# Measuring, rooting and first applying the next stage's layer norms inside each attention of the second layer

## The chip, the cores and the metric

The kernel runs on one core of one Trainium2 chip. The metric is the device time of one execution in microseconds (us). TensorE (PE) multiplies, VectorE (DVE), ScalarE (ACT) and GpSimd (POOL) do the rest, and SyncE (SP) issues transfers. Each engine works its own queue in order and meets the others at semaphores.

## The reference

Two pre-norm layers on x of 2 sequences x 2048 tokens x 256 features, float32. The first layer (16-head causal attention, then a mixture of 8 experts with two chosen) is not touched by the change. The second layer is

```python
x = x + _L1_attn_ref(_layernorm(x), L1_attn_W)      # returns n + softmax(causal(n K^T)) V, with K, V = n @ W.T and n the normed x
x = x + _L1_ffn_ref(_layernorm(x), W1, b1, W2, b2)  # relu(n @ Wq1.T + b1) @ Wq2.T + b2, the weights quantized to -1, 0, 1
```

with `_layernorm(x) = (x - mean) / sqrt(var + 1e-5)` over the 256 features of a token.

## The kernel before

x stays in SBUF as `X`, 32 rows of tiles: tile t holds 128 tokens, 16 tiles per sequence, in 4 blocks of 4 tiles (512 tokens). The second layer runs as five stages, each a block of the program behind a barrier of all engines:

1. keys of sequence 0 (`phase_keys(k, 0)`), 2. its attention (`phase_attend(k, 0)`), 3. keys of sequence 1, 4. its attention, 5. the MLP over the 8 blocks of both sequences (`phase_mlp`).

**A layer norm of a block** is made in three steps by three helpers. `norm_measure` (L224, L227): four BN_STATS and four BN_AGGR on DVE, which give mean and variance of the four tiles. `norm_root` (L233): one Sqrt on ACT. `norm_apply` (L239, L242): a reciprocal and four TENSOR_SCALARs on DVE, which write the normed tiles `xn`. Then PE turns them (8 transposes, L158, `turn`), ACT copies the result's high part out of PSUM (L165, `high_parts`) and DVE subtracts it for the low part (L171, `low_parts`); the matmuls take high and low parts.

**Keys of sequence 1.** For each block i PE multiplies the keys (12 matmuls into `ps_k`), turns block i+1, and multiplies the values (24 matmuls into `ps_v`). DVE's order is: norm 0, low parts 0, norm 1, and then for each i: low parts of the keys (L1872), low parts of the turned block i+1, the whole norm of block i+2. PE's turn of block i+2 waits for that norm. POOL adds the normed block into `X` (`residual`, L1791) and makes the low parts of the values (L1761). SP loads the key and value weights (`kv_hi`, `kv_lo`; PE waits for both before the first key matmul) and after them the MLP's raw weights. In sequence 0 ACT applies all blocks but the first; that stage is left as it is.

**Attention.** For each query tile q the scores are cut in parts of up to 4 key tiles. PE turns the first two parts of q's probabilities, multiplies the scores of q+1, and then weighs the values with q's parts. ACT makes the exponentials (L2060) and the high parts of the turned probabilities (L2069). DVE makes their low parts (`lows`, L2027), then the maxima of tile q+1's scores (`soften`, L2015 to L2022), in sequence 1 one step of the MLP's weight quantization (`ternary`), the row sum and its reciprocal, and at last adds the attended tile into `X` (L2049). In sequence 0's attention POOL adds the expert results into `X` for the 16 tiles of sequence 1.

**MLP.** It begins with the norm of block 0. In block i, ACT first takes the root of block i+1's norm, which waits for DVE's measurement, and then makes 8 high parts of the hidden layer (L2193) after a wait for the biases' load; DVE makes the full hidden values (L2222), POOL the low parts (L2176).

ACT holds the functions of one table set at a time; a load of another set is an instruction of its own (ACT_TABLE_LOAD). Exp and Sqrt lie in different sets here.

Of the kernel before, what the change touches and what calls it, by code (L numbers as in the profile page):

```python
# [15 lines left out]
P = 128  # L16
# [191 lines left out]

def layer_norm(k, mem, stem):


    nc = k["nc"]
    norm = {"X": k["X"], "eps": k["eps"], "k": k}
    for name, shape in (("stats", [P, 2, TB, 6]), ("moments", [P, 2, TB, 2]), ("std", [P, 2, TB]), ("rstd", [P, 2, TB])):
        norm[name] = mem.enter_context(nc.sbuf_tensor(f"{stem}_{name}", shape, F32))
    for name in ("stats_ok", "moments_ok", "std_ok", "rstd_ok", "xn_ok"):
        norm[name] = sem(k, f"{stem}_{name}")
    return norm


# [15 lines left out]
def norm_apply(dve, w, b, j, out, first=0):  # L236

    dve.wait_ge(w["std_ok"], b + 1)
    dve.reciprocal(w["rstd"][:, j], w["std"][:, j]).then_inc(w["rstd_ok"], 1)  # L239
    dve.wait_ge(w["rstd_ok"], b + 1)  # L240
    for t in range(TB):
# [29 lines left out]
def phase_qkv(k):  # L271
# [3 lines left out]
    with ExitStack() as mem:  # L275
# [24 lines left out]
        ps_n = ps("ps_n", [P, BT])  # L300
        norm = layer_norm(k, mem, "ln1")

# [673 lines left out]
def phase_tokens(k):  # L976
# [10 lines left out]
    with ExitStack() as mem:  # L987
# [79 lines left out]

        norm = layer_norm(k, mem, "ln2")
        x_turn = turner(k, "x2_turn", ps_t)
# [645 lines left out]
def phase_keys(k, b):  # L1715
# [3 lines left out]
    with ExitStack() as mem:  # L1719
# [10 lines left out]
        if b:  # L1730
# [32 lines left out]
        with nc.Block() as block:  # L1763
# [23 lines left out]
            def _(pool):  # L1787
                def residual(i):
                    x = k["X"][:, T0 + TB * i:T0 + TB * i + TB, :]
                    pool.wait_ge(norm["xn_ok"], i + 1)  # L1790
                    pool.tensor_tensor(x, x, xn[:, i], ALU.add).then_inc(k["residual_ok"], 1)  # L1791

# [12 lines left out]
            def _(act):  # L1805
# [3 lines left out]
                def root(i):  # L1809

                    norm_root(act, norm, i, i % 2)
                    if i and not b:
                        norm_apply_act(act, norm, i, i % 2, lambda t: xn[:, i, t:t + 1, :], T0, i)
# [34 lines left out]
            def _(dve):  # L1848
                def normed(i):
                    j = i % 2  # L1850
                    if not b:
                        if i == 0:
                            add_routed(dve, 0)
                        dve.wait_ge(sum_ok, 2 * i + 2)
                    norm_measure(dve, norm, i, j, T0)
                    if i and not b:
# [33 lines left out]
            def _(pe):  # L1890
                def turn(i):
                    pe.wait_ge(norm["xn_ok"], i + 1)
                    turn_block(pe, x_turn, i, lambda t, c: xn[:, i, t, c * P:(c + 1) * P])

# [25 lines left out]


CUTS = SEQ_TILES // 4
CUT = D * D_FF // P // CUTS


def phase_attend(k, b):

    nc, io = k["nc"], k["io"]
    with ExitStack() as mem:
# [3 lines left out]
        def ps(name, shape, dt=F32):  # L1933
# [26 lines left out]
        with nc.Block() as block:  # L1960
# [31 lines left out]
            def _(dve):  # L1992
# [31 lines left out]
                def lows(n):  # L2024
# [28 lines left out]
            def _(act):  # L2053
# [18 lines left out]
                for q in range(SEQ_TILES):  # L2072
# [56 lines left out]
def phase_mlp(k):  # L2129
# [3 lines left out]
    with ExitStack() as mem:  # L2133
# [14 lines left out]
        ps_t, ps_h, ps_y = ps("ps_x4", [P, DC, BT]), ps("ps_h4", [P, 3, BT]), ps("ps_y4", [P, TB, D])  # L2148
        norm = layer_norm(k, mem, "ln4")
        x_turn = turner(k, "x4_turn", ps_t)  # L2150
# [4 lines left out]
        with nc.Block() as block:  # L2155
# [128 lines left out]
def program(nc, io):  # L2284
# [12 lines left out]
    with ExitStack() as ctx:  # L2297
# [41 lines left out]
        first_ctx.close()  # L2339
        third_ctx, third_sems = semaphores(k)  # L2340
        half = 0
        for b in range(BATCH):
# [15 lines left out]
        mlp = len(third_sems)  # L2358
        k["stale"] = third_sems[half:] + [k["first_in"]]
        phase_mlp(k)  # L2360
        with nc.Block() as block:

            @block.gpsimd
            def _(pool):
                clear(pool, third_sems[mlp:])

# [32 lines left out]
```

## Time and profile before

| | us |
|---|---|
| median of 3 runs | 1761.5 |
| lowest and highest run | 1756.29 and 1763.25 |
| the profiled execution | 1764.49 |
| its span, first to last instruction | 1762.6 |

| engine | busy us | share of the span |
|---|---|---|
| PE | 1613.9 | 92% |
| DVE | 953.4 | 54% |
| ACT | 946.1 | 54% |
| POOL | 447.2 | 25% |

The profile's mean granted TensorE clock is 0.958 of full speed. A row of the time line gives start, duration, engine, line, operation and tiles, and in brackets the engine's idle time just before it and what ended it. A row of several instructions of one kind ends in their count.

### The profile page before, as it was taken

The page shows a single profiled execution, that of the slowest core. Times are in us where ns is not written, and L with a number is a line of the kernel's source. Part 1 is how long each engine was busy: PE and PEld are TensorE (multiplying, and loading weights), DVE is VectorE, ACT ScalarE, POOL GpSimd, SP SyncE. Part 2 cuts the span into 40 slices and gives each one's busy share as a digit, 9 for nine tenths or more (in the row PEclk, how much of TensorE's full clock was granted, in tenths as well). Part 3 has the DMA queues.
Part 4 walks back from the last instruction along what each step waited for, and adds up shares of the span by engine and source line. Part 5 has one row for each costly group of instructions (what it writes and reads, how often), then busy time and mean ns, then how long its engine had stood idle before and what let it go on. Part 6 is the DMA issues. An engine that isn't in the chain of part 4 may idle for free. (4 is left out here: it accounts for less than half of the span.)

```text
span 1762.6 us, 30806 instructions
## 1 busy us (share of the span) xinstructions
PE 1613.9 (92%) x10249; PEld 1111.8 (63%) x10250; DVE 953.4 (54%) x1846; ACT 946.1 (54%) x1521; POOL 447.2 (25%) x495
## 2 busy tenths in 40 slices
PE   6979999999999959998799999999579986997998
PEld 5833333333333337887678888888468976896887
DVE  6726566665554456777423333333356555655785
ACT  4779999999999933444222222222143434343432
POOL 0111121121111113555312222222343013001665
PEclk9989999999999978999899999999789988998999
DMA  7882855954732057213631111111312020000001
GB/s 230 232 219 87 216 141 128 235 128 126 154 64 41 19 167 288 93 63 136 204 107 48 54 48 54 48 51 51 130 36 73 1 72 1 1 1 4 25 24 48
DMA packets 88019, 169.40 MB, mean 96 GB/s; under 512 B 13504, under 2 KB 47808, under 8 KB 84768
## 3 DMA queue, kind: packets, MB, share of 16 engines
q1 hardware_dynamic: 80728, 146.90, 29.7%
q0 software_dynamic: 7056, 20.95, 3.6%
q8 instruction: 67, 1.10, 0.3%
q14 instruction: 40, 0.33, 0.1%
q10 hardware_dynamic: 128, 0.13, 0.0%
HBM read 96.67 MB, written 71.26 MB: 95 GB/s over the span
## 5 line engine op out<-in xcount | busy, mean ns | idle before, releaser
L836 ACT ACTIVATE probs<-ps_s 128x1024 f32<-128x1024 f32 (+3 forms) x640 | 511.7, 938 | 11.3 <-PE ps_s L902 8.3
L919 PE MATMUL ps_o<-probs,V 128*17 128x512 f32 (+3 forms) x2560 | 293.0, 536 | 1.6 <-POOL probs L824 1.2
L824 POOL TENSOR_SCALAR_AFFINE_SELECT probs<-probs 128x512 f32<-128x512 f32 x128 | 96.9, 763 | 427.5 <-ACT probs L836 426.4
L1638 DVE COPY slot_hT<-ps_hT 128x512 f32<-128x512 f32 x71 | 49.1, 692 | 196.7 <-PE ps_hT L1680 196.7
L902 PEld LDWEIGHTS ps_s<-Q_even,K_even 50*128 50x128 f32 x640 | 55.4, 186 | 133.4 <-ACT probs L836 119.9
L1688 PE MATMUL ps_slot_y<-we_out,slot_hT 128*128 x568 | 136.5, 384 | 2.2 <-issue 1.3
L2176 POOL TENSOR_TENSOR h_lo<-h,h_hi 128x512 fp32r<-128x512 f32 x64 | 89.4, 1414 | 178.9 <-DVE h L2222 178.9
L902 PEld LDWEIGHTS ps_s<-Q_odd,K_odd 50*128 50x128 f32 x640 | 54.9, 183 | 123.2 <-ACT probs L836 117.4
L902 PE MATMUL ps_s<-Q_even,K_even 50*128 50x512 f32 (+3 forms) x640 | 123.7, 444 | 8.9 <-DMA Q_even<-shift_parts 7.9
L902 PE MATMUL ps_s<-Q_odd,K_odd 50*128 50x512 f32 (+3 forms) x640 | 122.8, 439 | 0.3
L1599 POOL DMA_INDIRECT routed_rows<-slot_y,home_row x71 | 69.3, 977 | 176.4 <-ACT slot_y L1618 171.0
L2060 ACT ACTIVATE probs<-ps_s,neg_row_max 128x512 f32<-128x512 f32 (+2 forms) x80 | 49.4, 624 | 119.9 <-DVE neg_row_max L2022 119.9
L1688 PEld LDWEIGHTS ps_slot_y<-we_out,slot_hT 128*128 128x128 f32 x568 | 103.5, 192 | 14.7 <-issue 3.1
L874 DVE RECIPROCAL inv_denominator<-inv_denominator 128x512 f32<-128x512 f32 x32 | 107.3, 3353 | 1.1
L919 PEld LDWEIGHTS ps_o<-probs,V 128*17 128x17 f32 x2560 | 44.7, 95 | 85.6 <-issue 55.3
L1613 ACT ACTIVATE slot_xT_hi<-ps_xT 128x256 fp32r<-128x256 f32 x71 | 27.3, 384 | 123.0 <-PE ps_xT L1667 123.0
L1618 ACT ACTIVATE slot_y<-ps_slot_y 128x256 f32<-128x256 f32 x71 | 27.3, 384 | 108.0 <-PE ps_slot_y L1688 108.0
L141 PE MATMUL ps_o<-v_hi,pT_hi 128*128 128x256 f32 x272 | 80.8, 297 | 2.2 <-DVE pT_lo L2027 2.0
L1623 ACT ACTIVATE slot_silu<-ps_slot_mid 128x512 f32<-128x512 f32 x71 | 42.5, 598 | 71.0 <-PE ps_slot_mid L143 71.0
L1649 DVE TENSOR_TENSOR slot_h<-slot_silu,ps_slot_gated 128x512 f32<-128x512 f32 x71 | 48.8, 688 | 57.6 <-PE ps_slot_gated L143 57.6
L872 DVE COPY inv_denominator<-ps_o 128x512 f32<-128x512 f32 x32 | 22.1, 692 | 104.2 <-PE ps_o L933 104.2
L142 PE MATMUL ps_o<-v_lo,pT_hi 128*128 128x256 f32 x272 | 77.4, 284 | 0.0
(274 smaller groups left out, 3959.0 us busy)
## 6 DMA issues: line engine op xcount, KB each, us to landing
weight_parts<-weight_hi SPq DMA_DIRECT2D x20, 512.0 KB, 4.4
weight_parts<-weight_lo SPq DMA_DIRECT2D x20, 512.0 KB, 5.1
we_hi<-weight_parts SPq DMA_DIRECT2D x19, 512.0 KB, 5.9
we_lo<-weight_parts SPq DMA_DIRECT2D x19, 512.0 KB, 13.2
slot_rows<-slots_in SPq DMA_DIRECT2D x71, 128.5 KB, 2.1
qk_parts<-qk_hi SPq DMA_DIRECT2D x32, 256.0 KB, 4.6
qk_parts<-qk_lo SPq DMA_DIRECT2D x32, 256.0 KB, 5.3
we_hi<-attended_parts SPq DMA_DIRECT2D x16, 512.0 KB, 7.9
```

The source lines that it names most:

```text
L141: pe.matmul(out, lh, rh, start=start, stop=False)
L142: pe.matmul(out, lh, rl, start=False, stop=False)
L824: pool.affine_select(out=block_of, in_=block_of, compare_op=ALU.is_ge, fill=0.0, base=0, pattern=[[0, HG], [1, P]], channel_multiplier=-1) ...
L836: act.activation(probs[:, at % PROB_BUFS, 2 * p:2 * p + 2, off:BT], ps_s[:, s % SCORE_BUFS, :, off:BT], ACT.Exp).then_inc(exp_ok, 1)
L874: dve.reciprocal(inv[:, :], inv[:, :]).then_inc(norm_ok, 1)
L902: last = pe.matmul(ps_s[:, s % SCORE_BUFS, h, off:BT], K[j][HALF * h:HALF * h + USED_ROWS, p, t * P:(t + 1) * P], Q[j][HALF * h:HALF * h + ...
L919: last = pe.matmul(ps_o[32 * h:32 * h + DH + 1, s % 2, off:BT], k["V"][:, group, SEQ_TILES * b + t, h, :], probs[:, at % PROB_BUFS, h, off ...
L1599: pool.indirect_dma_start(out=io["routed"], out_offset=bass.IndirectOffsetOnAxis(ap=home[:, j], axis=0), in_=y[:, j, :], in_offset=None).t ...
L1638: dve.tensor_copy(hT[:, :, :], ps_h[:, :, :]).then_inc(hT_ok, 1)
L1688: last = pe.matmul(ps_y[:, :], hT[:, f], wo[:, bass.ds(e, 1), f, :], start=(f == 0), stop=(f == FC - 1))
L2060: act.activation(probs[:, q % 2, g * P:(g + m) * P], ps_s[:, g * P:(g + m) * P], ACT.Exp, bias=neg_top[:, q:q + 1], accum_out=chunk_total[ ...
L2176: pool.tensor_tensor(h_lo[:, j, f], h[:, f % 2], h_hi[:, j, f].bitcast(F32), ALU.subtract).then_inc(lo_ok, 1)
```

## The change

The variances of the next stage's blocks are measured inside the attention, where DVE has one measurement per query tile from q = 9 on: four in sequence 0's attention (for the four blocks of sequence 1), one in sequence 1's (for the MLP's block 0). ACT takes one root over all of them after its work of q = 13. DVE makes the reciprocals and applies the norm to the first block at q = 14, into a buffer `next_xn` that lives across stages. The keys stage of sequence 1 then has no measurement and no root, and DVE only applies blocks 1 to 3; the MLP begins with PE's turn of block 0. The sums that POOL makes on sequence 1's tiles are waited for before each measurement.

```diff
+def norm_scale(dve, w, j, out, row):
+
     for t in range(TB):
-        last = dve.tensor_scalar(out(t), w["X"][:, bass.ds(first + TB * b + t, 1), :], w["moments"][:, j, t, 0:1],
+        last = dve.tensor_scalar(out(t), w["X"][:, bass.ds(row + t, 1), :], w["moments"][:, j, t, 0:1],
                                  w["rstd"][:, j, t:t + 1], ALU.subtract, ALU.mult)
     last.then_inc(w["xn_ok"], 1)
...
-        norm = layer_norm(k, mem, f"ln3_{b}")
+        norm = k["next_norm"] if b else layer_norm(k, "ln3", norm_space(k, mem, "ln3", 2))
+
+        def xn_of(i):
+            return k["next_xn"][:, :, :] if b and i == 0 else xn[:, i]
...
                 def root(i):
 
+                    if b:
+                        return
                     norm_root(act, norm, i, i % 2)
...
                 def normed(i):
                     j = i % 2
-                    if not b:
-                        if i == 0:
-                            add_routed(dve, 0)
-                        dve.wait_ge(sum_ok, 2 * i + 2)
+                    if b:
+                        if i:
+                            dve.wait_ge(norm["rstd_ok"], 1)
+                            norm_scale(dve, norm, i, lambda t: xn[:, i, t:t + 1, :], T0 + TB * i)
+                        return
...
+MEASURE_AT, ROOT_AT, APPLY_AT = 9, SEQ_TILES - 3, SEQ_TILES - 2
...
+        following_norm = k["next_norm"] = layer_norm(k, "ln4" if b else "ln3_next", k["next_space"][b])
+        AHEAD, next_row = (1, 0) if b else (SEQ_BLOCKS, SEQ_TILES)
...
+                def next_applied():
+
+                    w = following_norm
+                    dve.wait_ge(w["std_ok"], 1)
+                    dve.reciprocal(w["rstd"][:, 0:AHEAD], w["std"][:, 0:AHEAD]).then_inc(w["rstd_ok"], 1)
+                    dve.wait_ge(w["rstd_ok"], 1)
+                    norm_scale(dve, w, 0, lambda t: k["next_xn"][:, t:t + 1, :], next_row)
...
                     for n in OF[q][2:]:
                         lows(n)
+                    if 0 <= q - MEASURE_AT < AHEAD:
+                        if not b:
+                            dve.wait_ge(summed, TOP_K * (q - MEASURE_AT + 1))
+                        norm_measure(dve, following_norm, q - MEASURE_AT, q - MEASURE_AT, next_row)
+                    if q == APPLY_AT:
+                        next_applied()
                     if b:
                         ternary(q)
...
+                    if q == ROOT_AT:
+                        w = following_norm
+                        act.wait_ge(w["moments_ok"], TB * AHEAD)
+                        act.activation(w["std"][:, 0:AHEAD], w["moments"][:, 0:AHEAD, :, 1], ACT.Sqrt, bias=k["eps"][:, 0:1]
+                                       ).then_inc(w["std_ok"], 1)
...
             @block.scalar
             def _(act):
-                norm_root(act, norm, 0, 0)
                 high_parts(act, x_turn, 0, lambda c: xT_hi[:, 0, c])
...
             @block.vector
             def _(dve):
-                norm_measure(dve, norm, 0, 0)
-                norm_apply(dve, norm, 0, 0, lambda t: xn[:, 0, t:t + 1, :])
-
...
-                    turn_block(pe, x_turn, i, lambda t, c: xn[:, j, t, c * P:(c + 1) * P])
+                    rows = k["next_xn"] if is_first(i) else xn[:, j]
+                    turn_block(pe, x_turn, i, lambda t, c: rows[:, t, c * P:(c + 1) * P])
```

The rest of the diff hands semaphores and buffers over between stages.

DVE's queue from the end of sequence 0's attention into the keys of sequence 1, before (the first row is the last addition into X of the attention):

```order
L2049 SCALAR_TENSOR_TENSOR X<-ps_o,inv_row_sum,X 128x256
L1960 UNCONDITIONAL_BRANCH
L1847 UNCONDITIONAL_BRANCH
L224 BN_STATS ln_1_stats<-X 128x6 x4
L227 BN_AGGR ln_1_moments<-ln_1_stats 128x2 x4
L239 RECIPROCAL ln_1_rstd<-ln_1_std 128x4
L242 TENSOR_SCALAR xn<-X,ln_1_moments,ln_1_rstd 128x256 x4
L171 TENSOR_TENSOR q3T_lo<-ps_x,q3T_hi 128x512 x2
L224 BN_STATS ln_1_stats<-X 128x6 x4
L227 BN_AGGR ln_1_moments<-ln_1_stats 128x2 x4
L239 RECIPROCAL ln_1_rstd<-ln_1_std 128x4
L242 TENSOR_SCALAR xn<-X,ln_1_moments,ln_1_rstd 128x256 x4
```

and in the change, from the same row:

```order
L2089 SCALAR_TENSOR_TENSOR X<-ps_o,inv_row_sum,X 128x256
L1986 UNCONDITIONAL_BRANCH
L1866 UNCONDITIONAL_BRANCH
L171 TENSOR_TENSOR q3T_lo<-ps_x,q3T_hi 128x512 x2
L255 TENSOR_SCALAR xn<-X,next_keys_moments,next_keys_rstd 128x256 x4
L1895 TENSOR_TENSOR k3T_lo<-ps_k,k3T_hi 128x512 x2
L171 TENSOR_TENSOR q3T_lo<-ps_x,q3T_hi 128x512 x2
L255 TENSOR_SCALAR xn<-X,next_keys_moments,next_keys_rstd 128x256 x4
```

The stage now begins with the low parts of block 0's turned tiles, and each later block has its four TENSOR_SCALARs alone.

ACT's queue in the change, around q = 13 and 14 of sequence 0's attention (probs is the exponential, pT_hi the high part of the turned probabilities):

```order
L2100 ACTIVATE probs,chunk_sum<-ps_s,neg_row_max 128x512
L2100 ACTIVATE probs,chunk_sum<-ps_s,neg_row_max 128x384
L2124 ACT_TABLE_LOAD
L2124 ACTIVATE next_keys_std<-next_keys_moments,eps 128x16
L2109 ACTIVATE pT_hi<-ps_p 128x512 x2
L2100 ACT_TABLE_LOAD
L2100 ACTIVATE probs,chunk_sum<-ps_s,neg_row_max 128x512
```

The two loads and the root stand where before the exponentials were followed by the two high parts at once. The same three rows are new in sequence 1's attention, while the load and root at the start of the keys stage and the load at the start of sequence 1's attention are gone.

DVE's queue in the change, at q = 14 of sequence 1's attention:

```order
L2053 TENSOR_TENSOR pT_lo<-ps_p,pT_hi 128x512
L2053 TENSOR_TENSOR pT_lo<-ps_p,pT_hi 128x384
L2060 RECIPROCAL next_mlp_rstd<-next_mlp_std 128x4
L255 TENSOR_SCALAR next_xn<-X,next_mlp_moments,next_mlp_rstd 128x256 x4
L2028 TENSOR_SCALAR below<-w_raw,half_gamma 128x512
L2082 TENSOR_REDUCE row_sum<-chunk_sum 128x1
L2085 RECIPROCAL inv_row_sum<-row_sum 128x1
L2089 SCALAR_TENSOR_TENSOR X<-ps_o,inv_row_sum,X 128x256
L2053 TENSOR_TENSOR pT_lo<-ps_p,pT_hi 128x512 x4
```

The reciprocal and the four TENSOR_SCALARs are new; they stand ahead of the quantization step, the row sum and the addition into X.

## Rows read from the trace of the kernel before

**Rows 1.** Stretches: length, PE, PEld, DVE, ACT, POOL busy, clock, DMA share, GB/s
```profile
1434.00:1482.80 48.80, 33.63 (x178) 29.60 (x179) 29.95 (x72) 23.42 (x42) 19.89 (x13) 0.82 0.18 65
1482.80:1608.50 125.70, 118.40 (x784) 107.91 (x784) 76.50 (x192) 46.76 (x121) 0.00 (x0) 0.96 0.00 1
1608.50:1632.50 24.00, 13.38 (x48) 10.21 (x48) 16.26 (x40) 9.22 (x15) 9.69 (x7) 0.79 0.03 6
```

**Rows 2.** Time line, start of the keys stage of sequence 1
```profile
1434.62 1.28 ACT L233 ACT_TABLE_LOAD   x1 [3.28 <-PEq L1960]
1434.66 1.41 DVE L224 BATCH_NORM_STATS2 ln_stats<-X 128x6 f32<-128x256 f32 x4 [0.32 <-PEq L1960]
1436.21 0.38 DVE L227 BATCH_NORM_AGGREGATE ln_moments<-ln_stats 128x2 f32<-128x6 f32 x4
...
1437.17 1.38 DVE L242 TENSOR_SCALAR xn<-X,ln_moments,ln_rstd 128x256 f32<-128x256 f32 x4
...
1438.61 1.97 PE L158 MATMUL ps_x<-ident,xn 128*128 128x128 f32 x8 [4.79 <-DVE xn L242]
...
1442.68 0.77 PE L141 MATMUL ps_k<-q3T_hi,kv_hi 128*128 128x512 f32 x1 [2.10 <-DVE q3T_lo L171]
```

**Rows 3.** DMA issues at 1435.00 and 1609.19: KB, us from issue to landing
```profile
kv_lo<-weight_parts SPq DMA_DIRECT2D x1, 512.0 KB, 4.5
```
```profile
b_rows<-b SPq DMA_DIRECT2D x1, 128.0 KB, 3.0
```

**Rows 4.** Time line, PE, DVE and POOL at the turns of blocks 2 and 3
```profile
1457.78 1.10 PE L158 MATMUL ps_x<-ident,xn 128*128 128x128 f32 x8 [2.89 <-DVE xn L242]
1468.92 1.96 PE L158 MATMUL ps_x<-ident,xn 128*128 128x128 f32 x8 [2.90 <-DVE xn L242]
```
```profile
1453.64 4.08 DVE L242 TENSOR_SCALAR xn<-X,ln_moments,ln_rstd 128x256 f32<-128x256 f32 x4
...
1464.77 4.09 DVE L242 TENSOR_SCALAR xn<-X,ln_moments,ln_rstd 128x256 f32<-128x256 f32 x4
```
```profile
1451.86 2.71 POOL L1761 TENSOR_TENSOR v_lo<-v_raw,v_hi 128x512 fp32r<-128x512 f32 x2 [10.88 <-ACT v_hi L1841]
1454.53 2.40 POOL L1791 TENSOR_TENSOR X<-X,xn 128x1024 f32<-128x1024 f32 x1
```

**Rows 5.** Stretches of 1 us, PE alone: length, busy, granted clock, DMA
```profile
1458.00:1459.00 1.00, 1.00 (x10) 0.86 0.00 0
...
1462.00:1463.00 1.00, 1.00 (x10) 0.93 0.00 0
...
1472.00:1473.00 1.00, 1.00 (x9) 0.81 0.00 0
```

**Rows 6.** Time line, start of the MLP
```profile
1608.86 1.40 DVE L224 BATCH_NORM_STATS2 ln_stats<-X 128x6 f32<-128x256 f32 x4 [0.32 <-PEq L1960]
...
1612.80 1.97 PE L158 MATMUL ps_x<-ident,xn 128*128 128x128 f32 x8 [4.79 <-DVE xn L242]
...
1618.90 0.30 ACT L233 ACTIVATE ln_std<-ln_moments,eps 128x4 f32<-128x4 f32 x1 [3.01 <-DVE ln_moments L227]
...
1619.11 0.67 ACT L2193 ACTIVATE h_hi<-ps_h,b_columns 128x512 fp32r<-128x512 f32 x1
```

**Rows 7.** Time line, sequence 1's attention: DVE at q = 9 and q = 14, ACT at q = 14
```profile
1543.42 0.48 DVE L2049 SCALAR_TENSOR_TENSOR X<-ps_o,inv_row_sum,X 128x256 f32<-128x256 f32 x1
1544.49 1.29 DVE L2027 TENSOR_TENSOR pT_lo<-ps_p,pT_hi 128x512 fp32r<-128x512 f32 x2 [0.58 <-ACT pT_hi L2069]
...
1547.05 0.69 DVE L2017 TENSOR_REDUCE chunk_max<-ps_s 128x1 f32<-128x512 f32 x1 [0.67 <-PE ps_s L143]
...
1599.14 0.48 DVE L2049 SCALAR_TENSOR_TENSOR X<-ps_o,inv_row_sum,X 128x256 f32<-128x256 f32 x1 [0.93 <-PE ps_o L143]
```
```profile
1586.96 1.09 ACT L2069 ACTIVATE pT_hi<-ps_p 128x512 fp32r<-128x512 f32 x2 [1.11 <-PE ps_p L2103]
1594.30 0.69 ACT L2060 ACTIVATE probs<-ps_s,neg_row_max 128x512 f32<-128x512 f32 x1 [6.25 <-DVE neg_row_max L2022]
```

More of the change, by code:

```diff
@@ L206, in _, with norm_space, layer_norm @@
             dve.tensor_copy(k["head_sel"][:, :], k["head_sum"][:, :]).then_inc(picked, 1)
[L209 to L215, printed above, removed]
+def norm_space(k, mem, stem, blocks):
+    return {name: mem.enter_context(k["nc"].sbuf_tensor(f"{stem}_{name}", [P, blocks, TB] + shape, F32))
+            for name, shape in (("stats", [6]), ("moments", [2]), ("std", []), ("rstd", []))}
+def layer_norm(k, stem, space):
+    norm = {"X": k["X"], "eps": k["eps"], "k": k, **space}
     for name in ("stats_ok", "moments_ok", "std_ok", "rstd_ok", "xn_ok"):
@@ L218, in layer_norm, with norm_parts @@
     return norm
+def norm_parts(norm):
+    return [norm[name] for name in ("stats_ok", "moments_ok", "std_ok", "rstd_ok", "xn_ok")]
 def norm_measure(dve, w, b, j, first=0):
@@ L240, in norm_apply @@
     dve.wait_ge(w["rstd_ok"], b + 1)
+    norm_scale(dve, w, j, out, first + TB * b)
+def norm_scale(dve, w, j, out, row):
     for t in range(TB):
-        last = dve.tensor_scalar(out(t), w["X"][:, bass.ds(first + TB * b + t, 1), :], w["moments"][:, j, t, 0:1],
+        last = dve.tensor_scalar(out(t), w["X"][:, bass.ds(row + t, 1), :], w["moments"][:, j, t, 0:1],
                                  w["rstd"][:, j, t:t + 1], ALU.subtract, ALU.mult)
@@ L300, in phase_qkv @@
         ps_n = ps("ps_n", [P, BT])
-        norm = layer_norm(k, mem, "ln1")
+        norm = layer_norm(k, "ln1", norm_space(k, mem, "ln1", 2))
         w_hi_ok, w_lo_ok, zero_ok, zero_out = sems(k, "qkv", "w_hi_ok w_lo_ok zero_ok zero_out")
@@ L1066, in phase_tokens @@
         ps_b = ps("ps_places", [P, TB + 1, EXPERTS])
-        norm = layer_norm(k, mem, "ln2")
+        norm = layer_norm(k, "ln2", norm_space(k, mem, "ln2", 2))
         x_turn = turner(k, "x2_turn", ps_t)
@@ L1790, in residual @@
                     pool.wait_ge(norm["xn_ok"], i + 1)
-                    pool.tensor_tensor(x, x, xn[:, i], ALU.add).then_inc(k["residual_ok"], 1)
+                    pool.tensor_tensor(x, x, xn_of(i), ALU.add).then_inc(k["residual_ok"], 1)
                 if b:
@@ L1809, in root @@
                 def root(i):
+                    if b:
+                        return
                     norm_root(act, norm, i, i % 2)
-                    if i and not b:
+                    if i:
                         norm_apply_act(act, norm, i, i % 2, lambda t: xn[:, i, t:t + 1, :], T0, i)
@@ L1850, in normed @@
                     j = i % 2
-                    if not b:
-                        if i == 0:
-                            add_routed(dve, 0)
-                        dve.wait_ge(sum_ok, 2 * i + 2)
+                    if b:
+                        if i:
+                            dve.wait_ge(norm["rstd_ok"], 1)
+                            norm_scale(dve, norm, i, lambda t: xn[:, i, t:t + 1, :], T0 + TB * i)
+                        return
+                    if i == 0:
+                        add_routed(dve, 0)
+                    dve.wait_ge(sum_ok, 2 * i + 2)
                     norm_measure(dve, norm, i, j, T0)
-                    if i and not b:
+                    if i:
                         norm_shift(dve, norm, i, j)
@@ L1892, in turn @@
                     pe.wait_ge(norm["xn_ok"], i + 1)
-                    turn_block(pe, x_turn, i, lambda t, c: xn[:, i, t, c * P:(c + 1) * P])
+                    turn_block(pe, x_turn, i, lambda t, c: xn_of(i)[:, t, c * P:(c + 1) * P])
                 turn(0)
@@ L2148, in phase_mlp @@
         ps_t, ps_h, ps_y = ps("ps_x4", [P, DC, BT]), ps("ps_h4", [P, 3, BT]), ps("ps_y4", [P, TB, D])
-        norm = layer_norm(k, mem, "ln4")
+        norm = k["next_norm"]
         x_turn = turner(k, "x4_turn", ps_t)
@@ L2340, in program @@
         third_ctx, third_sems = semaphores(k)
+        k["next_xn"] = ctx.enter_context(nc.sbuf_tensor("next_xn", [P, TB, D], F32))
+        k["next_space"] = [norm_space(k, ctx, "next_keys", SEQ_BLOCKS), norm_space(k, ctx, "next_mlp", 2)]
         half = 0
@@ L2358, in program @@
         mlp = len(third_sems)
-        k["stale"] = third_sems[half:] + [k["first_in"]]
+        in_use = norm_parts(k["next_norm"])
+        k["stale"] = [handle for handle in third_sems[half:] if all(handle is not used for used in in_use)] + [k["first_in"]]
         phase_mlp(k)
@@ L2364, in _ @@
             def _(pool):
-                clear(pool, third_sems[mlp:])
+                clear(pool, third_sems[mlp:] + in_use)
         second_ctx.close()
```

## The prediction

> **What bounds the kernel now.** I looked first at the stretches [rows 1]. In sequence 1's attention PE is busy 118.40 of 125.70 us at a clock of 0.96: that stage is PE's, and DVE (76.50) and ACT (46.76) have room. The keys stage before it is another matter: PE works 33.63 of 48.80 us at a mean clock of 0.82, and in the first 24 us of the MLP 13.38 us at 0.79. These two stretches hold the norms that the change takes out. So the question has two halves: what does PE wait for there, and does the work, put into the attentions, stay in DVE's and ACT's idle time?
>
> The time line of the keys stage's start [rows 2] shows the first wait. DVE begins to measure at 1434.66, right behind the barrier, and PE begins to turn only at 1438.61, after 4.79 us idle that end with DVE's xn; the first key matmul follows at 1442.68. The MLP begins the same way [rows 6]: DVE at 1608.86, PE at 1612.80. Then the turns of blocks 2 and 3 [rows 4]: PE stands 2.89 and 2.90 us, both for DVE's xn, whose four instructions take 4.08 and 4.09 us there against 1.38 in [rows 2]. Last the clock behind those two waits [rows 5].
>
> **The change part by part.**
>
> *Start of the keys stage.* Measure, root, reciprocal and apply, 1438.61 - 1434.66 = 3.95 us, go from PE's path. But PE's first key matmul also needs both halves of the key weights, and their load is issued at the stage's start: kv_lo, issued at 1435.00, lands 4.5 us later, at 1439.5 [rows 3]. Turning from 1434.66 on, with the 1442.68 - 1438.61 = 4.07 us that turn, high and low parts take, would be ready at 1438.7. The load is late next, so the first key matmul moves from 1442.68 to 1439.5: **3.2 us**. The transfer's bounds: 3.95 if it should land earlier, 2.2 if it slips by 1 us. Whether PE is at half or full clock there I leave as it is: PE still waits some 3 us for the load.
>
> *Waits of the turns of blocks 2 and 3.* DVE no longer measures blocks 1 to 3 in this stage. The norm of block 2 loses measurement (1.41 + 0.38), the wait for the root, and the reciprocal: from the first measurement to the first apply that is 1437.17 - 1434.66 = 2.5 us [rows 2], here 2.4 of it count, since DVE took the measurement right behind the low parts of block 1. So the apply, at 1453.64 before, can start 2.4 us earlier against PE's work. What does it cost itself? The four took 1.38 alone and 4.08 beside POOL, which had a 2.40 us addition and low parts of 2.71 / 2 = 1.36 each in the same time [rows 4]. PE wants block 2 about 2.4 + 4.08 - 2.89 = 3.6 us after the new start. At 1.38 there is room, at one low part more (2.7) there is too, at 4.08 a wait of 0.5 remains. I take none, since POOL's long addition of block 1 stands behind both value parts of block 0 and so comes later than the apply. Block 3 is as block 2. **2.89 + 2.90 = 5.8 us**.
>
> *The clock behind these waits.* After the turn of block 2 PE is busy throughout, but the granted clock is 0.50 from about 1458.7 to 1462.1 [rows 5]: 0.28 us of the first slice, 3 whole ones between the rows, and 0.14 of the last, 3.4 us at 1.2 instead of 2.4 GHz, which loses 1.7. After the turn of block 3 it is low until 1472.4, again 3.4 us and 1.7. Ahead of each fall PE had stood 2.9 us. Without these waits PE works without a gap from the first key matmul on, and I expect no fall: **3.4 us**. Bounds: 0 and 3.4.
>
> *The stage's end* is not changed: PE's last values, ACT's high parts and POOL's low parts follow PE. The keys stage gives 3.2 + 5.8 + 3.4 = 12.4.
>
> *Start of the MLP.* PE turns at 1608.86 instead of 1612.80: 3.94 us. Two things can be late there: the biases, issued at 1609.19 and landing at 1612.2 [rows 3], and block 1's measurement, whose root ACT must take ahead of its first hidden part (root at 1618.90, h_hi at 1619.11 [rows 6]). Shifted by 3.94 that hidden part is due at 1615.2. DVE's wait for the biases ends at 1612.2, measurement 1.9, root 0.3: 1614.5, in time. The table load now stands behind the high parts and the wait for the biases, 1612.2 + 1.28 = 1613.5, and the root needs it at 1614.1: hidden. The mean clock in this stretch is 0.79 [rows 1]; PE now stands in two pieces, 0.8 and 2.1 us, not 4.8 and 2.0, and may lose less. Between 0 and 1.3 I take 0.5. **4.4 us**.
>
> *What the attentions take on.* Five measurements of 1.41 + 0.38 + 0.1 = 1.9 us on DVE. The tightest place is q = 9 of sequence 1, where the quantization step already fills DVE: the addition into X at 1543.42 shows no wait, the low parts behind it 0.58, the second maximum 0.67 [rows 7]. Of 1.9 us, 0.58 goes into the first gap; the low parts come 1.3 late, ending at 1547.1 instead of 1545.8, but PE wants them only after the scores of tile 11, of whose three parts the second is done just at 1547.05; the maxima behind them take up 0.67 per part and are level again at the third. No cost. The apply (0.2 + 1.38 = 1.6 us) at q = 14 has 0.93 + 0.58 = 1.5 us of gap in sequence 1; behind it stand the low parts of q = 15, with no scores to cover them: 0.1 us lost, and in sequence 0, with no quantization step, none. On ACT the root with its load is 1.28 + 0.30 = 1.6 us, in front of a high part that waited 1.11 [rows 7]: 0.5 late, covered by the same scores. The load of the Exp table falls into the 6.25 us wait of the next exponential [rows 7]. POOL's sums were done long before q = 9. Two loads at stage starts go (1.28 each, beside other work, worth nothing). **-0.1 us**, between -3 and 0; if the scores did not cover them, see the third rival.
>
> **Sum.** 12.4 + 4.4 - 0.1 = 16.7 us. The profiled execution took 1764.5, so it would be 1747.8; against the median of the runs, 1761.5, 1744.8. I give 1745. A measurement of this kernel can tell about 0.5%, 8.8 us.
>
> **The rivals.**
>
> *The applies still collide and the clock still falls (21%).* If each apply goes on taking 4.08 us, block 2 and block 3 leave 0.5 us each, and if the clock falls all the same (the stage has a new wait of some 3 us ahead of its first key matmul), the 3.4 go: 16.7 - 1.0 - 3.4 = 12.3, 1749.2; with another 2 us at half clock for the first keys, 1751. For it: the 4.08 and 4.09 [rows 4]. Against: the other partner is now a 1.36 us low part. The Trainium skill's page SBUF — State Buffer, "Who interferes with whom", says that a VectorE instruction in a two-port mode and a GpSimd instruction exclude each other for a whole instruction, whoever comes first; the four instructions for 4.08 us beside a 2.40 us addition agree. By that rule each of them could wait once more for a POOL instruction in its way, which is this case's 0.5 us per block.
>
> *Only the two starts are gained (7%).* The turns of blocks 2 and 3 could have a second cause behind DVE's, such as ACT, which has 1.9 us of weight sums after blocks 1 and 2. Then 3.2 + 4.4 = 7.6 remain: 1754.
>
> *The inserted work lies on the attentions' path (6%), slower.* The mechanism: DVE's low parts and ACT's high parts are what PE weighs with; if the cover of the scores is thinner than read, each insertion at q = 9 to 14 stops PE. Its price: 5 x 1.9 + 2 x 1.6 on DVE and 4 x 1.28 + 2 x 0.3 on ACT, 18.4 us, against 16.7 gained: 1763; where PE's clock falls behind each as behind the waits in [rows 4, 5], 1.7 each for five more, 1772. It decides from about 90% of the insertions on. Against it: the gaps of 0.58, 0.67, 1.11 and 6.25 [rows 7] and the score parts that PE has still to do there. The Trainium skill's page ScalarE: Activation LUTs, "Table sets: the hidden batching unit", advises to "do all the exps together, then all the sqrts", and "What ACT_TABLE_LOAD costs" prices a switch at 2.66 us with its drain; the change does the opposite, with four switches inside the exponentials and two fewer elsewhere, and by that price the four would be 10.6 instead of 5.1 us, this rival 1768. The rows show the load alone at 1.28.
>
> **How the numbers follow.** Forecast 66%, the rivals 21, 7 and 6%. Only a new measurement's own spread adds to this: the three runs reach from 1756.3 to 1763.3. The range goes from 1739 (the forecast with the load landing in time, 0.8, the rest of the MLP's clock, 0.8, full clock at the first keys, up to 2.6, and a low run) up to 1753, past the first rival, leaving out the second and third and some of the tails. Faster by over 0.5% means under 1752.7: the forecast, nearly all of the first rival and a little of the second, 85%. Within 0.5%: most of the second and half of the third, 11%. Slower by over 0.5%: 4%.
>
> **What would show it.** In the changed profile: PE's first turn at the barrier plus 0.1 us in both stages; the first key matmul about 5 us behind the barrier, held by no DVE wait; no wait of 2.9 us at the turns of blocks 2 and 3 and a clock of 1.0 behind them; the keys stage near 36.5 us instead of 48.8; sequence 1's attention still 125.7 us. Attentions longer by over 2 us each, or a clock under 0.9 in the later keys stage, would make it wrong.

## The result, and the profile after

The changed kernel takes 1746.3 us in the median (4 runs, 1744.14 to 1748.7), the kernel before 1762.34 in the same comparison: a ratio of 0.9917, 95% interval 0.989 to 0.9943, 14.6 us faster by the ratio. In a second comparison the ratio was 0.9918 (0.9896 to 0.9939). The forecast was 1745 (1739 to 1753).

The profiled execution took 1748.7 us, its span is 1747.0 against 1762.6. Its stretches, in the columns of [rows 1] (length, PE, PEld, DVE, ACT, POOL busy, clock, DMA share, GB/s):

```profile
1432.50:1468.30 35.80, 28.62 (x178) 25.54 (x179) 17.21 (x31) 21.05 (x36) 20.24 (x13) 0.90 0.25 89
1468.30:1594.90 126.60, 120.03 (x784) 109.33 (x784) 79.34 (x205) 48.19 (x123) 0.00 (x0) 0.95 0.00 1
1594.90:1618.90 24.00, 15.19 (x55) 11.62 (x56) 15.49 (x33) 8.70 (x14) 11.07 (x8) 0.82 0.03 7
```

The keys stage of sequence 1 is most of the story: 35.8 us where 48.8 stood, DVE down from 29.95 to 17.21 us, the mean clock up from 0.82 to 0.90. First all of PE's waits in that stage (who waited for whom: us in total, times, longest), then its turns and its first key matmul in the time line:

```profile
PE ps_k L141 <- DMA kv_lo<-weight_parts: 4.4, 1, 4.4
PE ps_s L141 <- PEq L1780: 2.7, 1, 2.7
PE ps_x L158 <- PEq L1986: 0.8, 1, 0.8
```
```profile
1432.60 1.06 PE L158 MATMUL ps_x<-ident,next_xn 128*128 128x128 f32 x8 [0.85 <-PEq L1986]
1438.07 0.80 PE L141 MATMUL ps_k<-q3T_hi,kv_hi 128*128 128x512 f32 x1 [4.40 <-DMA kv_lo<-weight_parts]
1443.12 1.04 PE L158 MATMUL ps_x<-ident,xn 128*128 128x128 f32 x8
1449.59 1.04 PE L158 MATMUL ps_x<-ident,xn 128*128 128x128 f32 x8
1456.06 1.03 PE L158 MATMUL ps_x<-ident,xn 128*128 128x128 f32 x8
```

PE turns 0.05 us behind the barrier, and then waits for the weights' load and, but for the barriers at the stage's two ends, for nothing else: the turns of blocks 2 and 3, which waited 2.89 and 2.90 us [rows 4], have no idle time in front. DVE's applies of these two blocks, and POOL beside the first:

```profile
1446.03 2.35 DVE L255 TENSOR_SCALAR xn<-X,next_keys_moments,next_keys_rstd 128x256 f32<-128x256 f32 x4
...
1452.50 2.36 DVE L255 TENSOR_SCALAR xn<-X,next_keys_moments,next_keys_rstd 128x256 f32<-128x256 f32 x4
```
```profile
1446.75 2.77 POOL L1778 TENSOR_TENSOR v_lo<-v_raw,v_hi 128x512 fp32r<-128x512 f32 x2 [11.68 <-ACT v_hi L1860]
1449.48 2.38 POOL L1808 TENSOR_TENSOR X<-X,xn 128x1024 f32<-128x1024 f32 x1
```

2.35 us instead of 4.08: they now run beside POOL's low parts of 1.4 us each, and its 2.4 us addition begins only when the apply has ended.

The MLP's start did not come out as forecast. ACT, DVE and PE there:

```profile
1600.58 1.28 ACT L241 ACT_TABLE_LOAD   x1 [3.20 <-DVE next_mlp_moments L235]
1601.88 0.30 ACT L241 ACTIVATE next_mlp_std<-next_mlp_moments,eps 128x4 f32<-128x4 f32 x1
1602.08 1.82 ACT L2237 ACTIVATE h_hi<-ps_h,b_columns 128x512 fp32r<-128x512 f32 x3
```
```profile
1598.57 1.41 DVE L232 BATCH_NORM_STATS2 next_mlp_stats<-X 128x6 f32<-128x256 f32 x4 [0.36 <-DMA b_rows<-b]
```
```profile
1595.19 1.07 PE L158 MATMUL ps_x<-ident,next_xn 128*128 128x128 f32 x8 [0.84 <-PEq L1986]
...
1603.59 0.80 PE L2312 MATMUL ps_h<-x4T_hi,w_ternary 128*128 128x512 f32 x1 [2.25 <-DVE h L2263]
...
1610.48 1.97 PE L158 MATMUL ps_x<-ident,xn 128*128 128x128 f32 x8 [2.44 <-DVE xn L255]
```

The load of the Sqrt table does not run behind the high parts: it waits until DVE's measurement of block 1 ends (1600.50) and then keeps the root and the hidden parts behind it 1.28 us back; PE, at full clock until 1603.3, has made three hidden tiles and stands 2.25 us.

**Where the time went, stage by stage.** One profile cannot be set against one other here, since the program ahead of the change, nearly the same code in every kernel, reached the first masking of scores in sequence 0's attention at 1310.2 us in the profile before, at 1307.1 after, and between 1298.0 and 1310.2 over all profiles. So I measured every profile of this study between fixed instructions: keys stage, from the last addition into X of sequence 0's attention to the first masking of scores in sequence 1's; opening, from there to the addition of the third tile; rest of the attention, from there to the sixteenth; MLP, from there to the span's end.

| kernel profiled | seq. 0, tiles 3 to 16 | keys stage | opening of seq. 1 | seq. 1, tiles 3 to 16 | MLP |
|---|---|---|---|---|---|
| before | 110.33 | 50.51 | 13.94 | 109.74 | 154.55 |
| before, again | 110.31 | 50.19 | 13.92 | 109.72 | 154.55 |
| changed | 110.33 | 37.42 | 15.46 | 109.72 | 152.61 |
| changed, again | 110.38 | 37.38 | 15.46 | 109.71 | 152.59 |
| keys_only | 110.34 | 37.50 | 15.46 | 109.71 | 156.11 |
| mlp_only | 110.35 | 47.24 | 13.93 | 109.74 | 151.14 |
| inserted_only | 110.38 | 47.21 | 13.93 | 109.64 | 155.38 |
| residual_last | 110.29 | 52.37 | 13.93 | 109.76 | 155.86 |
| early_table | 110.40 | 38.01 | 13.92 | 109.76 | 151.19 |
| kv_kept | 110.40 | 34.57 | 15.46 | 109.68 | 151.32 |
| both | 110.42 | 34.54 | 13.92 | 109.69 | 150.59 |
| measured_5x | 125.84 | 36.34 | 15.45 | 109.81 | 150.89 |
| apply_last | 110.57 | 37.47 | 13.92 | 110.51 | 150.91 |

Between the two compared profiles: 13.1 us from the keys stage, 1.9 from the MLP, nothing from the inserted work, 1.5 lost in the opening of sequence 1's attention, and 2.1 gained before the keys stage by code that does the same in both.

### The profile page after: what moved, and what is told of

It is laid out like the page before. It is cut to its first block and busy times, and to the rows that moved or that the text cites. A ratio compares the mean times of both kernels' runs of the same rounds, so it can differ in the third digit from the quotient of the medians.

```text
span 1747.0 us, 30802 instructions
## 1 busy us (share of the span) xinstructions
PE 1610.0 (92%) x10249; PEld 1108.5 (63%) x10250; DVE 946.7 (54%) x1843; ACT 947.3 (54%) x1520; POOL 446.9 (26%) x495
## 5 line engine op out<-in xcount | busy, mean ns | idle before, releaser
L1701 PEld LDWEIGHTS ps_slot_y<-we_out,slot_hT 128*128 128x128 f32 x568 | 103.2, 191 | 14.6 <-issue 3.2
L1662 DVE TENSOR_TENSOR slot_h<-slot_silu,ps_slot_gated 128x512 f32<-128x512 f32 x71 | 48.8, 688 | 57.6 <-PE ps_slot_gated L143 57.6
```

The costliest lines, as they stand in the source:

```text
L1701: last = pe.matmul(ps_y[:, :], hT[:, f], wo[:, bass.ds(e, 1), f, :], start=(f == 0), stop=(f == FC - 1))
```

## The experiments

**Each half alone.** keys_only leaves the MLP with its own first norm and inserts nothing in sequence 1's attention:

```diff
-        norm = k["next_norm"]
+        norm = layer_norm(k, "ln4_own", norm_space(k, mem, "ln4", 2))
...
+                norm_root(act, norm, 0, 0)
                 high_parts(act, x_turn, 0, lambda c: xT_hi[:, 0, c])
...
+                norm_measure(dve, norm, 0, 0)
+                norm_apply(dve, norm, 0, 0, lambda t: xn[:, 0, t:t + 1, :])
```

> The changed kernel with only the half for the keys stage: measured, rooted and first applied inside sequence 0's attention; nothing inserted in sequence 1's attention, MLP with its own norm as before. Theory (each stage gives back its own waits, the attentions are free): the keys stage of sequence 1, from its barrier to the first score matmul, takes 35.8 us instead of 48.2, so the kernel is 12 to 13 us faster than before. Rival (the 4 us at the MLP's start and the inserted work make up a larger part): 8 us or less.

Measured: 1747.24 us in the median against 1759.53, ratio 0.9923 (0.9901 to 0.9946), 12.3 us by the medians. The theory holds: the interval begins at 9.5 us, above the rival's 8.

mlp_only is the counterpart: `norm = layer_norm(k, f"ln3_{b}", ...)` and the old `root` and `normed` in the keys stage, nothing inserted in sequence 0's attention.

> The changed kernel with only the half for the MLP: one measurement, root and apply inside sequence 1's attention; keys stage with its own norms as before. Theory: 2 to 3.5 us faster than before, not the 4.4 of my sum, because the load of the Sqrt table now waits behind the measurement of block 1 (1.28 us on the path). Rival (the profile's MLP was only unlucky with the clock): 4 to 5 us faster.

Measured: 1757.04 us, ratio 0.9985 (0.9969 to 1.0001), 2.5 us by the medians, inside what I expected but not to be told from zero by the total alone. Its MLP took 151.14 us, against 154.55 to 156.11 in the five profiles with the old start. So the half is worth 3 to 5 us where it acts, and the MLP alone does not tell my 2 to 3.5 us from the rival's 4 to 5; the mean over all profiles, further down, is 3.7. The two halves, 12.3 + 2.5 = 14.8, come near the 14.6 of the whole.

**The inserted work alone.** In sequence 0's attention all of it is done and not used; both following stages make their own norms. The diff is that of both halves above, with the insertions kept for `not b` only.

> All of sequence 0's inserted work (four measurements, root with two table loads, reciprocal and apply at q = 9 to 14) is done and its result not used; keys stage and MLP make their own norms as before, sequence 1's attention has nothing inserted. Theory (the insertions lie in gaps): the same time as before within 0.5 us. Rival (they lie on the path): 4 x 1.9 + 1.6 + 2.9 = 12 us slower.

Measured: 1758.02 us against 1759.53, ratio 0.9993 (0.9977 to 1.001), and 110.38 us between the third and the sixteenth tile against 110.33. The insertions are free to within 0.1 us; the rival's 12 us are excluded. How they are taken in shows at q = 14 in the changed kernel, ACT of sequence 0's attention:

```profile
1409.52 1.28 ACT L2124 ACT_TABLE_LOAD   x1
1410.82 0.31 ACT L2124 ACTIVATE next_keys_std<-next_keys_moments,eps 128x16 f32<-128x16 f32 x1
1411.03 1.07 ACT L2109 ACTIVATE pT_hi<-ps_p 128x512 fp32r<-128x512 f32 x2
1412.11 1.28 ACT L2100 ACT_TABLE_LOAD   x1
1417.95 0.69 ACT L2100 ACTIVATE probs<-ps_s,neg_row_max 128x512 f32<-128x512 f32 x1 [4.56 <-DVE neg_row_max L2048]
```

The second load takes 1.28 us of a wait that is still 4.56 us long behind it. In sequence 1, whose own insertion is one measurement and one apply, DVE's addition into X at q = 9, which the forecast held for the tightest place, came 1.8 us late and the next tile's on time, the one at q = 14 came 0.66 us late and the next tile's on time; the low parts behind the latter had been waiting for ACT (0.58) anyway.

**How much room there was.** With a busy share of 55% one could think that DVE takes anything. measured_5x repeats the BN_STATS of the four measurements four more times, with the results left unused in a buffer that is free once POOL's sums are done, hence the added wait (POOL's last sum ended at 1343.5, the first inserted group began at 1355.8):

```diff
+                        if not b:
+                            dve.wait_ge(summed, TOP_K * SEQ_BLOCKS)
+                        for n in range(0 if b else 4 * TB):
+                            at = next_row + TB * (q - MEASURE_AT) + n % TB
+                            dve.bn_stats(back[:, 0, q - MEASURE_AT, 6 * n:6 * n + 6], k["X"][:, at:at + 1, :])
                         norm_measure(dve, following_norm, q - MEASURE_AT, q - MEASURE_AT, next_row)
```

> The changed kernel; at q = 9 to 12 of sequence 0's attention DVE makes each of the four BN_STATS five times (16 more at each q, 5.6 us, their results left unused), so 7.5 us stand where 1.9 us stood. Theory (the scores of the next tile and DVE's small gaps cover an insertion, some 3 us of it in all, the rest reaches PE): each of the four costs 4 to 5 us, the third to sixteenth tile of that attention take 126 to 130 us instead of 110.4. Rival (DVE has far more room, its busy share says 55%): under 4 us in all.

Measured: 125.84 us for tiles 3 to 16, 15.5 us more than 110.33, or 3.9 per insertion; the total is back at 1761.97 (ratio 1.0001 against the kernel before, 0.998 to 1.0023). One repeated group took 5.31 us:

```profile
1355.80 5.31 DVE L2079 BATCH_NORM_STATS2 next_back<-X 128x6 f32<-128x256 f32 x16
```

That is a little less than the 4 to 5 us that I had expected and far from the rival's 4 in all. The whole gain of the change can be lost in this one place. PE alone over tiles 3 to 16 (length, busy, clock, DMA), in the changed kernel and in measured_5x:

```profile
1321.46:1431.79 110.33, 107.99 (x736) 1.00 0.09 30
```
```profile
1311.37:1437.21 125.84, 113.84 (x736) 0.96 0.08 26
```

Of the 15.5 us 9.7 are idle time of PE. In the other 5.9 the same 736 matmuls took longer: the clock, at full speed throughout in the changed kernel, was at half for three stretches of 3.4 us, each behind a wait for DVE's low parts, which makes 5.1. So of an insertion of 5.3 + 1.9 = 7.2 us about 2.4 reach PE as a wait and 4.8 are taken in, and PE's slower work behind the waits adds 1.5. The room per query tile, read so, is about 4.8 us, or 3.3 if that loss is charged to it; the change uses 1.9. Both figures come from insertions of one size: where between 1.9 and 7.2 us the cost begins was not tried.

apply_last moves the reciprocal and the apply from q = 14 to q = 15 (`APPLY_AT = SEQ_TILES - 1`), where no scores follow.

> The changed kernel with the reciprocal and the apply at q = 15 instead of q = 14 of both attentions, behind the last low parts. Theory (there the last addition into X waits 1.5 us for PE in sequence 0 and 0.9 in sequence 1, and 1.6 us are put in front of it): the stages' ends come 0.1 to 0.3 us later in sequence 0 and 0.7 to 0.9 in sequence 1, about 1 us in all. Rival (anything in the last tile goes straight on the path): 1.6 us in each.

Measured: tiles 3 to 16 took 110.57 us in sequence 0 (+0.24) and 110.51 in sequence 1 (+0.79), both as expected; the total, 1746.33 (0.9926, 0.9895 to 0.9957), is the changed kernel's. DVE at the end of sequence 1:

```profile
1591.28 1.38 DVE L255 TENSOR_SCALAR next_xn<-X,next_mlp_moments,next_mlp_rstd 128x256 f32<-128x256 f32 x4
1592.57 0.75 DVE L2030 SCALAR_TENSOR_TENSOR w_ternary<-w_raw,half_gamma,below 128x512 fp32r<-128x512 f32 x1
...
1593.69 0.48 DVE L2089 SCALAR_TENSOR_TENSOR X<-ps_o,inv_row_sum,X 128x256 f32<-128x256 f32 x1
```

The last addition shows no wait for PE any more: there the inserted 1.6 us have used up the gap.

**POOL's part in the waits.** residual_last is the kernel before with POOL's queue in another order:

```diff
+                for i in range(SEQ_BLOCKS if b else 0):
+                    v_rest(pool, i)
                 for i in range(SEQ_BLOCKS):
                     residual(i)
-                    if b:
-                        v_rest(pool, i)
```

> The kernel before, with one thing changed: in the keys stage of sequence 1 POOL makes the low parts of all values first and the additions of the normed blocks into X after them, as a reordering of its queue. Theory (PE's two waits of 2.9 us are in part made by POOL's 2.4 us addition that holds up DVE's apply): the applies take 2.4 instead of 4.08 us, the two waits shrink to about 1.2 us each, 3 to 7 us faster, the clock behind them deciding how much; less what the additions at the stage's end then cost (three of 2.4 us behind the last low part, up to 7 us). Rival (the norm is simply late, POOL has no part): waits of 2.9 stay.

Measured: 1763.68 us, ratio 1.0029 (1.0014 to 1.0043), 4 us slower. In it (DVE, then PE, then POOL):

```profile
1450.01 2.05 DVE L242 TENSOR_SCALAR xn<-X,ln_moments,ln_rstd 128x256 f32<-128x256 f32 x4
```
```profile
1452.12 1.09 PE L158 MATMUL ps_x<-ident,xn 128*128 128x128 f32 x8 [0.86 <-DVE xn L242]
```
```profile
1471.63 9.23 POOL L1791 TENSOR_TENSOR X<-X,xn 128x1024 f32<-128x1024 f32 x4
```

The mechanism holds: without the addition beside it the apply takes 2.05 instead of 4.08 us, PE's wait shrinks from 2.89 to 0.86, and the clock did not fall behind either of the two. The time I had expected, 3 to 7 us less, did not come. What I had weighed too lightly is the end: four additions of 2.3 us, 9.2 in all against the 7 that I had allowed, come behind the last low part, and the next stage's barrier waits for all of them; the first masking of scores follows PE's last value matmul by 13.5 us instead of 4.4. So of each 2.9 us wait some 2 us were POOL's and 0.9 the late norm's; the change removed both: the applies start earlier, and the additions come behind them.

**The next waits.** early_table puts one instruction at the head of the MLP, so that the Sqrt table is loaded while PE turns:

```diff
+                act.activation(norm["std"][:, 1, 0:1], k["eps"][:, 0:1], ACT.Sqrt)
                 high_parts(act, x_turn, 0, lambda c: xT_hi[:, 0, c])
```

> The changed kernel with one more ACT instruction at the head of the MLP: a Sqrt of a single column, whose table load runs while PE turns block 0. Theory (the load behind block 1's measurement is what kept the MLP's gain at 1.9 instead of 4.4 us): the first hidden part comes 1.28 us earlier against the barrier, PE's wait of 2.25 us for h shrinks to about 1, and the kernel is 1 to 2.5 us faster than the changed one, 17 to 18 us faster than before. Rival (POOL's low parts set the pace of block 0): no change against the changed kernel.

Measured: 1747.55 us, ratio 0.9921 (0.9899 to 0.9943) against the kernel before, where the changed kernel on the same chip had 0.9918: no difference in the total. In the profile the step does what it says:

```profile
1595.08 1.28 ACT L2228 ACT_TABLE_LOAD   x1 [3.26 <-PEq L1986]
1596.37 0.20 ACT L2228 ACTIVATE next_mlp_std<-eps 128x1 f32<-128x1 f32 x1
...
1600.53 0.30 ACT L241 ACTIVATE next_mlp_std<-next_mlp_moments,eps 128x4 f32<-128x4 f32 x1 [2.98 <-DVE next_mlp_moments L235]
1600.73 0.67 ACT L2238 ACTIVATE h_hi<-ps_h,b_columns 128x512 fp32r<-128x512 f32 x1
```

The first hidden part starts 6.42 us behind the last addition into X instead of 7.69. PE's wait for h is 0.57 us instead of 2.25. The MLP takes 151.19, where the changed MLP took 150.89 to 152.61 in six profiles (mean 151.6), which alone says little. These six differ in where the clock fell around the turn of block 1. In the two profiles of the changed kernel it fell there as in early_table, just before that turn and again some 7 us later, 3.4 us each, and against these two the MLP is 1.4 us shorter: the 1.28 us arrive. The pair both and kv_kept, alike in their clock too, differs by 0.7. The expectation of 1 to 2.5 us is not borne out by the total, which cannot tell 1 us; the stage speaks for some 0.7 to 1.4 us and against the rival, on four profiles.

kv_kept loads the key and value weights once, for both sequences, into memory that is free until sequence 1's attention:

```diff
-        w_hi, w_lo = sb("kv_hi", [P, DC, 2 * D], F32R), sb("kv_lo", [P, DC, 2 * D], F32R)
+        w_hi, w_lo = [k["mlp_ternary"][0][:, n, :].rearrange("p (c n) -> p c n", c=DC) for n in range(2)]
...
                 turn(0)
-                pe.wait_ge(w_in, 32)
+                if not b:
+                    pe.wait_ge(w_in, 32)
```

> The changed kernel with the key and value weights loaded once, in sequence 0's keys stage, into memory that the MLP's quantized weights take over only in sequence 1's attention; sequence 1's keys stage has no load and no wait for one. Theory (the load ends the wait before the first key matmul, 4.40 us idle): the first key matmul starts about 3 us behind the barrier instead of 5.5, 2.3 us faster or more than the changed kernel, up to 4.5 if the clock does not fall. Rival (turn, high and low parts are as late as the load): no change.

Measured: 1745.55 us, ratio 0.9902 (0.9875 to 0.9928), 2.1 us under the changed kernel by the medians. The stage shows it beyond doubt, 34.57 us instead of 37.4:

```profile
1434.18 1.06 PE L158 MATMUL ps_x<-ident,next_xn 128*128 128x128 f32 x8 [0.85 <-PEq L1987]
1437.25 0.52 PE L141 MATMUL ps_k<-q3T_hi,w_ternary 128*128 128x512 f32 x1 [2.01 <-DVE q3T_lo L171]
```

The first key matmul comes 3.1 us behind the turn instead of 5.5, and waits for the low parts now.

> The changed kernel with both: early Sqrt table load at the MLP's head and key and value weights kept. Theory: the two gains add, 3.5 to 7 us faster than the changed kernel, 19 to 22 faster than before.

Measured: 1744.2 us (1740.44 to 1746.95), ratio 0.9903 (0.9882 to 0.9923), 3.4 us under the changed kernel's 1747.64 by the medians, just under the 3.5 to 7 that I expected, and 17 us under the kernel before, where I expected 19 to 22. Its ratio is that of kv_kept, so the totals show no gain from the early load on top. The intervals of the ratios overlap; that it beats the changed kernel rests on the keys stage (34.54 against 37.4 us) more than on the totals.

> The changed kernel once more, on the same chip as its three variants: 14 to 17 us faster than before; the keys stage again 35.8 us long, the MLP 151 to 152 us from its barrier to the end.

Measured: 1747.64 us, 0.9918, 14.4 us faster by the ratio and 13.8 by the medians; keys stage 37.38 and MLP 152.59 by the table's bounds, each within 0.05 us of the first profile.

**The clock behind the two waits.**

> The kernel before, once more, for a second profile of it. Theory (which of the two waits of 2.9 us in the keys stage the clock falls behind is a matter of the execution, since two kernels with the same stage showed a fall behind one of them alone): again two waits of 2.9 us; the keys stage 47.2 us with one fall or 50.5 with two. Rival: both falls belong to the kernel before, 50.5 again.

Measured: 1759.67 us; the keys stage took 50.19 us, and PE again turned slowly behind the second wait:

```profile
1451.37 1.30 PE L158 MATMUL ps_x<-ident,xn 128*128 128x128 f32 x8 [2.89 <-DVE xn L242]
1462.53 1.97 PE L158 MATMUL ps_x<-ident,xn 128*128 128x128 f32 x8 [2.90 <-DVE xn L242]
```

For this kernel my expectation of a fall by chance failed: both of its profiles have two falls, and 50.2 to 50.5 us. But mlp_only and inserted_only have the same stage with the same two waits (2.88 and 2.90, 2.88 and 2.91 us), and take 47.24 and 47.21. In mlp_only the second wait is followed by a turn at full clock:

```profile
1465.90 1.10 PE L158 MATMUL ps_x<-ident,xn 128*128 128x128 f32 x8 [2.90 <-DVE xn L255]
```

The missing fall explains 1.7 of the 3.3 us. The rest, which my expectation of one fall or two left out, lies at the first keys, where the clock was still at half (PE: length, busy, clock, DMA; the kernel before, then mlp_only):

```profile
1442.68:1448.49 5.81, 5.81 (x15) 0.50 0.38 125
```
```profile
1441.20:1444.16 2.96, 2.96 (x7) 0.50 0.61 217
```

So a wait of 2.9 us does not by itself decide whether the clock falls. What does, the runs leave open: the two kernels differ from the kernel before in what surrounds the stage, and each was profiled once.

## Why the prediction was right

The likeliest case came out, by most of its steps and nearly by its sum: 16.7 us forecast, 14.6 measured by the ratio, 16.0 by the first medians and 13.8 by the later ones. That the two profiles differ by 15.6 us is in part luck: 2.1 of them arose ahead of the change, and the terms erred both ways.

- *Start of the keys stage, 3.2 us.* Right in what is late next: the weights' load. Its size was read too short. kv_lo took 5.1 us to land instead of 4.5, and the first key matmul came 5.5 us behind the barrier, not 4.9. From 8.1 us behind the barrier to 5.5 the step gave 2.6 us.
- *Waits of blocks 2 and 3, 5.8 us.* Right. I had found room for an apply of 1.38 us and for one of 2.7, a POOL low part more, and it took 2.35. The first rival's 4.08 us did not come, and its remaining waits of 0.5 us neither.
- *The clock behind these waits, 3.4 us.* Right against the profile before, where the clock fell twice. But the clock gave 4.8 us there, not 3.4. From the first key matmul to the first masking of scores, PE alone, before and changed:

```profile
1442.68:1484.37 41.69, 33.17 (x176) 0.83 0.05 18
```
```profile
1438.07:1469.21 31.14, 28.41 (x176) 0.92 0.15 54
```

  Added up between the points where the clock changes, that is 14.4 us at half clock before and 4.75 after. Of the 9.6 us between them 6.8 are the two falls; 1.1 lie at the first keys (5.81 and 4.75 us) and 1.75 at the first scores, which the low clock now reaches only behind the masking. Half of each is time: 3.4 + 0.5 + 0.9. The sum had nothing for the last two. With the start's 2.5 and the waits' 5.8 this makes the 13.1 us of the table. Against other profiles it is less: the same old stage in two other kernels ran 3.0 to 3.3 us shorter, with the second fall missing and a shorter low stretch at the first keys. Over the four profiles with the old stage (mean 48.8) and the six with the new one and its load (mean 37.4) the stage gave 11.4 us, not 12.4. Behind its first key matmuls the stage ran without a fall up to the barrier, as said.
- *Start of the MLP, 4.4 us.* The gain at the start is there, 11.06 us from the last addition to the first hidden part against 7.69, 3.4. The step that failed is "The table load now stands behind the high parts and the wait for the biases ... hidden": it stood behind the wait for the measurement, and its 1.28 us were on the path. I had taken from ACT's queue that the load waits for the biases. At the end of the MLP 1.9 us were left in the compared profiles, 3.7 between the means of five old and six new ones (155.3 and 151.6). What the compared pair lost lies between the turns of blocks 1 and 2, 17.7 us apart before and 19.0 after, with 3.4 and 6.4 us at half clock: there the clock took it, not the load.
- *What the attentions take on, 0.1 us.* Right, 0.0. The slower rival had the cover of the scores thinner than read; measured_5x puts it at 3.3 to 4.8 us per tile, against 1.9 used.
- *Not in the sum:* the opening of sequence 1's attention lost 1.5 us in both profiles of the changed kernel. There the clock stayed low longer, 13.7 us on end, where it was 10.2 before and 6.8 in apply_last. PE alone, the eighth to tenth microsecond behind the first masking, in the changed kernel and in apply_last:

```profile
1477.21:1479.21 2.00, 1.22 (x6) 0.50 0.00 0
...
1481.21:1483.21 2.00, 2.00 (x8) 0.50 0.00 0
```
```profile
1477.26:1479.26 2.00, 0.78 (x7) 1.00 0.00 0
```

  It did so in five of the eight profiles with the new keys stage and in none of the five with the old one. I left this stage out because nothing in it was changed.

## What to carry to other kernels

Work that starts a stage can be hidden at the end of the stage before, if the room is read per iteration, from the gap in front of each next instruction and not from the busy share: at 55% busy DVE took in 1.9 us per tile here for nothing, while 7.2 us cost PE 2.4 in waits and 1.5 more in slower work behind them. Before moving it, find what is late next: here it was the weights' load, and keeping the weights gave 2.4 us more at that place. And look at what shares the moved instructions' time: two thirds of each wait of 2.9 us came from POOL's addition beside the apply, and vanished here because the apply moved ahead of it.

## What the runs showed of the hardware

- A table load on ACT stood directly ahead of the instruction that it serves, and whether it waited with it depended on the instruction's waits. At a stage's start before, where the root has one wait, the load ran at once behind the barrier and the root began 0.72 us behind it [rows 2]; so did the load at 1412.11 above, 4.56 us ahead of its exponential. In the changed MLP the root comes behind two waits, for the biases and for the measurement. The one for the measurement shows as an entry of its own in ACT's queue (L240, until 1600.55), and the load began behind it, 0.08 us after the measurement's end. A one-column Sqrt ahead of the waits brings it forward by a whole 1.28 us.
- A change of table set cost ACT the load's 1.28 us and nothing more that shows: the last exponential's accumulator read ended at 1409.50, the load began at 1409.52, the root at 1410.82. The Trainium skill's page ScalarE: Activation LUTs, "What ACT_TABLE_LOAD costs", counts 2.66 us with a drain; no drain shows here, on an engine that had just ended its work.
- Four TENSOR_SCALARs of 128x256 took 1.38 us alone, 2.05 to 2.36 beside a 1.3 to 1.4 us POOL instruction, and 4.08 beside a low part and a 2.4 us addition. The Trainium skill's page SBUF — State Buffer, "Who interferes with whom", has a VectorE instruction in a two-port mode and a GpSimd instruction exclude each other for a whole instruction. The steps of 0.7 to 1 us beside the short one and 2.7 beside the two agree with that; that these instructions ran in such a mode, no run here shows.
- TensorE's clock behind the same wait of 2.9 us fell to 1.2 GHz in some profiles and stayed at 2.4 in others, each fall 3.4 us long and so worth 1.7. Together with the other low stretches this made 3.3 us of difference in the keys stage of one and the same code, 1.5 in the opening of the attention and up to 1.7 in the MLP (152.6 and 150.9 us, with 6.4 and 3.4 us at half clock between the turns of blocks 1 and 2). In measured_5x it fell behind waits of 2.50, 1.54 and 1.80 us and not behind one of 1.78; behind residual_last's two of 0.9 us it did not fall. With 12 us of spread ahead of the change, a single pair of profiles tells a gain of 15 us only if it is taken apart by stages.
